# A bias table without its last column, and attention steps weighed two at a time

## The reference

```python
xn = layernorm(x)                                # no scale, no shift
# attention, 16 heads of width 32
q, k, v = heads(xn @ Wq.T), heads(xn @ Wk.T), heads(xn @ Wv.T)
attn = softmax(q @ k.T * 512 ** -0.5)
rel_idx = arange(S)[:, None] - arange(S)[None, :] + (S - 1)      # S = 1024
attn = attn + bias_table[rel_idx]                # added after the softmax
s = layernorm(attn @ v) * gamma + beta
# feed forward, with a spiking neuron of 5 steps behind it
h = square(relu(xn @ W_fc.T))
g = silu(spikes(h @ W_proj.T) / 5)
out = x + s * g
```

## Time and profile before

| | before |
|---|---|
| median of 3 runs | 3528.83 us (3526.05 to 3529.1) |
| span of the profiled execution | 3528.6 us |
| TensorE busy (matmul) | 3421.4 us, 97% |
| ScalarE busy | 2624.2 us, 74% |
| VectorE busy | 2506.6 us, 71% |
| GpSimd busy | 1720.5 us, 49% |
| attention stage | from about 1391 us on |

### The profile page before, as it was taken

How to read it: one execution, slowest core, us unless ns; L and a number is a source line. 1 busy time by engine, 2 the same in 40 slices (tenths; PEclk the granted TensorE clock), 3 DMA queues, 4 the chain that set the end, 5 groups by cost and what they waited for, 6 DMA issues and landing times.

```text
span 3528.6 us, 55344 instructions
## 1 busy us (share of the span) xinstructions
PE 3421.4 (97%) x19961; PEld 1441.3 (41%) x19964; DVE 2506.6 (71%) x4051; ACT 2624.2 (74%) x3898; POOL 1720.5 (49%) x998
## 2 busy tenths in 40 slices
PE   7999999999999999999999999999999999999996
PEld 3444444444444444433433433433433433433431
DVE  5555555555555555777888888888888888888887
ACT  6433333333333335999999999999999999999997
POOL 0012222111111123899666666666666666666672
PEclk9999999999999999999999999999999999999999
DMA  5122322333222222222322322322322322322322
GB/s 186 57 80 80 104 79 80 101 96 103 80 79 79 81 83 86 83 67 72 121 88 84 95 87 83 96 87 84 96 85 83 98 85 82 100 85 82 100 61 84
DMA packets 238752, 312.35 MB, mean 89 GB/s; under 512 B 96624, under 2 KB 132208, under 8 KB 238480
## 3 DMA queue, kind: packets, MB, share of 16 engines
q1 hardware_dynamic: 238480, 308.82, 28.2%
HBM read 174.65 MB, written 76.61 MB: 71 GB/s over the span
## 4 chain that ended last, share of the span: by engine, by line
ACT 33%; PE 11%; issue 10%; DVE 4%; SPq 1%; DMA 1%; ACTq 0%; POOL 0%; DVEq 0%; POOLq 0%
ACT recurrence_or_probs L1457 17%; ACT s_sb L1464 16%; PE misc L1331 3%; PE acc L1406 3%; PE s_ps L1386 3%; PE s_ps L1372 2%; DVE s_sb L1533 2%; DMA xT<-xnT 1%; SPq L322 1%; DVE gate_or_tokens L1662 0%; PE misc L1313 0%; DVE outT L1553 0%; DVE x_or_queries L1570 0%; DVE gate_or_tokens L1665 0%; PE s_ps L1331 0%
## 5 line engine op out<-in xcount | busy, mean ns | idle before, releaser
L1739 POOL TENSOR_TENSOR recurrence_or_probs<-recurrence_or_probs,toep 128x512 f32<-128x512 f32 (+1 forms) x375 | 1288.5, 3457 | 366.5 <-ACT recurrence_or_probs L1457 366.2
L1533 DVE TENSOR_SCALAR_CACHE_REDUCE s_sb<-s_ps 128x1024 f32<-128x1024 f32 x998 | 1213.7, 1220 | 353.8 <-PE s_ps L1372 325.7
L1464 ACT ACTIVATE s_sb<-s_sb,nmax 128x1024 f32<-128x1024 f32 x998 | 1167.0, 1169 | 9.8 <-DVE s_sb L1533 9.5
L1457 ACT ACTIVATE recurrence_or_probs<-s_ps 128x1024 f32<-128x1024 f32 x1024 | 1060.1, 1036 | 7.7 <-PE s_ps L1386 7.5
L559 PE MATMUL ps_fc<-xnT_part,w_fc 128*128 128x512 f16 x3072 | 707.2, 380 | 4.5 <-DVE w_fc L817 4.5
L574 PE MATMUL ps_y<-w_pr,hid_part 128*128 128x512 f16 x3072 | 706.2, 380 | 3.6 <-issue 2.6
L740 ACT ACTIVATE relu<-ps_fc 128x512 f32<-128x512 f32 x256 | 152.7, 597 | 626.9 <-PE ps_fc L559 626.9
L130 POOL TENSOR_TENSOR recurrence_or_probs<-gate_or_tokens,beta_row 128x512 f32<-128x512 f32 x60 | 89.9, 1499 | 1035.3 <-DVE gate_or_tokens L185 1031.7
L929 DVE TENSOR_TENSOR hid<-relu 128x512 f32<-128x512 f32 x256 | 210.3, 822 | 510.9 <-ACT relu L740 510.9
L1406 PE MATMUL acc<-recurrence_or_probs,val 128*32 128x512 f32 x4096 | 545.2, 604 | 2.2 <-DVE recurrence_or_probs L1649 1.5
L559 PEld LDWEIGHTS ps_fc<-xnT_part,w_fc 128*128 128x128 f16 x3072 | 300.6, 98 | 369.3 <-issue 7.8
(11 more groups left out here) (180 smaller groups left out, 2685.1 us busy)
## 6 DMA issues: line engine op xcount, KB each, us to landing
toep<-table_rows SPq DMA_DIRECT2D x32, 2048.0 KB, 8.3
x_or_queries<-x_or_queries SPq DMA_DIRECT2D x384, 64.0 KB, 2.0
x_or_queries<-in_x SPq DMA_DIRECT2D x16, 1024.0 KB, 10.4
xnT<-xnT_part SPq DMA_DIRECT2D x32, 512.0 KB, 8.5
x_or_gate<-in_x SPq DMA_DIRECT2D x16, 1024.0 KB, 9.2
base<-x_or_gate SPq DMA_DIRECT2D x16, 1024.0 KB, 6.8
xT<-xnT SPq DMA_DIRECT2D x32, 512.0 KB, 9.7
result<-gate_or_tokens SPq DMA_DIRECT2D x64, 256.0 KB, 2.0
```

What stands on the lines that cost most here:

```text
L1457: nc.scalar.activation(prob[:, k % PROBS, 2 * second:2 * second + 2, :].rearrange("p j n -> p (j n)"), s_ps[:, item_buffer(pair_item(m)), ...
L1464: nc.scalar.activation(s_sb[:, i % 4, :], s_sb[:, i % 4, :], ACT.Exp, bias=nmax[:, par, j, st:st + 1], scale=-1.0, accum_out=den[:, par, j ...
L1533: nc.vector.tensor_scalar(s_sb[:, i % 4, :], s_ps[:, item_buffer(tile_item(n)), :], -1.0, None, ALU.mult, ALU.min, accum_out=nmax[:, par, ...
L1739: nc.gpsimd.tensor_tensor(tile, tile, toep[:, par, :, at:at + width], ALU.add).then_inc(biased, 1)
```

## The change

The bias of the far keys is taken out of the table: the last column is subtracted from all columns, and the widened part is zero. Its share of the output is then the same for all queries of a batch: the far value times the sum of all values, which is the sum of all tokens times `Wv`. VectorE sums the tokens of each chunk in the feed-forward stage (`sum_tokens`), and 48 small products in slot 0 make the values of all batches and groups (`sum_values`, `take_far_values`); the prefix sums go. The table is grown ahead of the first normalisation and lies in the buffer of relu and its square.

Steps are weighed two at a time, in the second half step of odd steps. Key blocks have a new order in both halves (`KEY_ORDER`), so the added bias widths by step become 512, 128, 512, 256, 512, 384, 512, 512 and then 0, 128, 0, 256, 0, 0, 384, 512 (before 128, 256, 384, 512, 512, 512, 512, 512 and 0, 0, 0, 0, 128, 256, 384, 512). Value projections, the parts of the query and key projection, the rows, one output transpose and the two copies of `acc` have new half steps. The buffers of scores for the sums go from four to three, and the last chunk's gate and base are loaded into `xT`.

```diff
+SUM_TOKENS_AT = {10: 0, 12: 1}
...
-        relu = sb("relu", [P, 2, 512], F32)
-        hid = sb("hid", [P, 2, 512], F32)
+        hidden = sb("hidden_or_table", [P, 2, 2, 512], F32)
+        relu, hid = hidden[:, 0], hidden[:, 1]
...
-        table = sb("table", [rows, d["table_ext"].shape[1]], F32)
+        table = hidden.rearrange("p i a n -> p (i a n)")[:rows, :d["table_ext"].shape[1]]
+        far_row = sb("far_row", [rows, 1], F32)
...
                 wait(sp, xt_stored, (c - 1) * 32)
+                wait(sp, tokens_summed, (c - 1) * 2)
...
-                    sp.wait_ge(table_grown, 1)
-                    sp.dma_start(d["table_ext"], table[:]).then_inc(table_loaded, 16)
-                    sp.wait_ge(table_loaded, 32)
+                    sp.wait_ge(table_stored, 16)
...
             load_x(0)
+            sp.dma_start(table[:, :known], d["tableT"]).then_inc(table_loaded, 16)
             for q in range(4):
                 sp.dma_start(pieces[q], d["fcT"].rearrange("(k p) n -> p k n", p=P)[:, :, q * BANK:(q + 1) * BANK]).then_inc(loaded[q], 16)
+            sp.wait_ge(table_grown, 3)
+            sp.dma_start(d["table_ext"], table).then_inc(table_stored, 16)
             for k in range(4):
                 sp.dma_start(staged[4 + k], d["prT"].rearrange("(k p) n -> p k n", p=P)[:, 4 * k:4 * k + 4]).then_inc(loaded[4 + k], 16)
-            sp.dma_start(table[:, :known], d["tableT"]).then_inc(table_loaded, 16)
...
+                    if n == 0:
+                        act.wait_ge(table_stored, 16)
                     nc.scalar.activation(relu[:, f % 2, :], ps_fc[:, f % 2, :], ACT.Relu).then_inc(relu_done, 1)
...
             def grow_table():
                 dve.wait_ge(table_loaded, 16)
-                nc.vector.tensor_copy(table[:, known:], table[:, known - 1:known].broadcast_to([rows, table.shape[1] - known])
-                                      ).then_inc(table_grown, 1)
+                nc.vector.tensor_copy(far_row[:], table[:, known - 1:known]).then_inc(table_grown, 1)
+                nc.vector.memset(table[:, known:], 0.0).then_inc(table_grown, 1)
+                dve.wait_ge(table_grown, 1)
+                nc.vector.tensor_scalar(table[:, :known], table[:, :known], far_row[:, 0:1], None,
+                                        ALU.subtract).then_inc(table_grown, 1)
+
+            def sum_tokens(c, par, part):
+
+                if part == 0 and c == 0:
+                    dve.wait_ge(xt_hi, 4)
+                    dve.wait_ge(xt_lo, 4)
+                elif part == 0:
+                    dve.wait_ge(xt_turned, c * TURNED)
+                nc.vector.tensor_reduce(spiking.token_sums[:, c * 2 + part, :], xnT[:, par, part], AX,
+                                        ALU.add).then_inc(tokens_summed, 1)
...
+                    if f in SUM_TOKENS_AT:
+                        sum_tokens(c, par, SUM_TOKENS_AT[f])
...
             statistics(0)
+            grow_table()
             normalise(0)
...
-            grow_table()
             chunks(dve, chunk, NC - 2)
...
-VALUES = {0: (0, 0), 2: (0, 1), 4: (1, 0), 6: (1, 1)}
-QUERY_KEYS = {12: (0, 0), 14: (0, 1), 16: (1, 0), 18: (1, 1), 20: (2, 0), 22: (2, 1), 24: (3, 0), 26: (3, 1)}
-SUM_VALUES, ROWS_1, ROWS_0, OUT_1, OUT_0 = 8, 10, 27, 28, 30
+VALUES = {0: (0, 0), 1: (0, 1), 5: (1, 0), 6: (1, 1)}
+QUERY_KEYS = {12 + 4 * u + i: (u, i) for u in range(4) for i in range(3)}
+QK_PARTS = 3
+FAR_VALUES, ROWS_1, ROWS_0, OUT_1, OUT_0 = 9, 10, 28, 29, 30
+KEY_ORDER = ((4, 0, 5, 1, 6, 2, 7, 3), (0, 4, 1, 5, 2, 3, 6, 7))
+COPY_1, COPY_0 = 4, 20
...
+COPIES = 3
...
-        s_sb = sb("s_sb", [P, 4, S], F32)
+        s_sb = sb("s_sb", [P, COPIES, S], F32)
+        last_gate = xT.rearrange("p a k s -> p (a k s)").bitcast(F32).rearrange("p (t i e) -> p t i e", t=4, i=2)
...
         def bias_width(k):
 
-            return min(512, (k % 8 + 1) * P - k // 8 * 512)
+            return min(512, (key_block(k) + 1) * P - k // 8 * 512)
...
-        def last_weighed(b, hg, h):
-
-            k = h // 2 - WEIGH_LAG
-            return (b, hg, k) if k >= 0 else (*before(b, hg), SLOT_STEPS + k)
+        def weighed_at(b, hg, k):
+
+            ready = (k - WEIGH_LAG, k - WEIGH_LAG + 1) if k % 2 else ()
+            return [(b, hg, i) if i >= 0 else (*before(b, hg), SLOT_STEPS + i) for i in ready]
...
-                for n in range(part * 6, part * 6 + 6):
+                for n in range(part * 4, part * 4 + 4):
...
-            def sum_values(s):
+            def sum_values():
 
                 take_misc()
-                pe.wait_ge(consts, CONSTS)
-                pe.wait_ge(v_read, s.g * 2 + 2)
-                for t in range(TB - 1):
-                    last = nc.tensor.matmul(misc[:, :TB], val[:, s.par, t, :], before_key[:, t, :],
-                                            start=(t == 0), stop=(t == TB - 2))
-                last.then_inc(pre_ps, 1)
-                last_use[0] = (pre_read, s.g + 1)
+                pe.wait_ge(sums_split, 3)
+                for hg in range(HG):
+                    for n, (k, a, bb) in enumerate((k, a, bb) for k in range(EB) for a, bb in TERMS):
+                        last = nc.tensor.matmul(misc[:, hg * NB:(hg + 1) * NB], w["v"][:, bb, k, hg * P:(hg + 1) * P],
+                                                batch_parts[:, a, :, k], start=(n == 0), stop=(n == 11))
+                last.then_inc(far_ps, 1)
+                last_use[0] = (far_made, 1)
...
                     if second and (s.main if k >= WEIGH_LAG else s.prev):
-                        weigh(*last_weighed(b, hg, h))
+                        for done in weighed_at(b, hg, k):
+                            weigh(*done)
...
-                wait(dve, sum_done, n - 3)
+                wait(dve, sum_done, n - COPIES + 1)
...
-            def copy_acc(g, par, half):
+            def copy_acc(g, half):
 
                 dve.wait_ge(pv_done, g * 16 + half * 8 + 8)
-                dve.wait_ge(pre_read, g + 1)
+                dve.wait_ge(far_made, 1)
                 wait(dve, tr_ps, g * 2 + half - 1)
-                nc.vector.tensor_tensor(outT[:, half, :].rearrange("p (q n) -> p q n", q=4),
-                                        acc[:].rearrange("p (q n) -> p q n", q=4),
-                                        prefix[:, par, half * 4:half * 4 + 4].unsqueeze(2).broadcast_to([P, 4, P]),
+                nc.vector.tensor_scalar(outT[:, half, :], acc[:], far_values[:, g % HG, g // HG:g // HG + 1], None,
                                         ALU.add).then_inc(acc_read, 1)
...
-                    if h == 2 * WEIGH_LAG and s.prev:
-                        copy_acc(s.g - 1, 1 - s.par, 1)
-                    if h == 2 * WEIGH_LAG + 16 and s.main:
-                        copy_acc(s.g, s.par, 0)
+                    if h == COPY_1 and s.prev:
+                        copy_acc(s.g - 1, 1)
+                    if h == COPY_0 and s.main:
+                        copy_acc(s.g, 0)
```

More of the change, by code:

```diff
@@ L1183, in item_release, with key_block, bias_from @@
             return p_done, m + 1
+        def key_block(k):
+            return KEY_ORDER[k // 8][k % 8]
         def bias_width(k):
-            return min(512, (k % 8 + 1) * P - k // 8 * 512)
+            return min(512, (key_block(k) + 1) * P - k // 8 * 512)
+        def bias_from(k):
+            return TW - P - key_block(k) * P + k // 8 * 512
         def add_count(g, k):
-            return g * 12 + (k + 1 if k < 8 else k - 3)
+            return g * 12 + sum(bias_width(i) > 0 for i in range(k + 1))
         def added_late(g, k):
@@ L1378, in score_pair @@
                 x = pair_item(s.g * 32 + 2 * k + second)
-                half, tb = k // 8, k % 8
-                if tb == 0 and second == 0:
+                half, tb = k // 8, key_block(k)
+                if k % 8 == 0 and second == 0:
                     pe.wait_ge(rows_loaded[half], s.g * 64 + 64)
@@ L1548, in copy_acc, with split_sums @@
-            def copy_acc(g, par, half):
+            def split_sums():
+                sums = spiking.token_sums.rearrange("p (b i) k -> p b k i", b=NB)
+                nc.vector.tensor_reduce(batch_sums[:], sums, AX, ALU.add).then_inc(sums_split, 1)
+                dve.wait_ge(sums_split, 1)
+                nc.vector.tensor_copy(batch_parts[:, 0], batch_sums[:]).then_inc(sums_split, 1)
+                dve.wait_ge(sums_split, 2)
+                nc.vector.tensor_tensor(batch_parts[:, 1], batch_sums[:], batch_parts[:, 0], ALU.subtract).then_inc(sums_split, 1)
@@ L1706, in slot @@
                         finish_statistics(NB * 2 - 2, LAST_STATISTICS[h])
[L1709 to L1712 removed]
+            split_sums()
             slots(dve, slot)
@@ L1715, in _ @@
             newton(NB * 2 - 2)
-            copy_acc(NG - 1, (NG - 1) % 2, 1)
+            copy_acc(NG - 1, 1)
             finish_normalise(NB * 2 - 2, 0)
@@ L1733, in add_bias @@
                     return
[L1734 removed]
+                at = bias_from(k)
                 if k == 0:
```

74 lines of the change are left out of this document (38 added, 36 removed).

## The result

The changed kernel takes 3597.39 us (median of four runs, 3594.62 to 3606.93) against 3527.94 before: a ratio of 1.0202, 95% interval 1.0187 to 1.0216. It was slower, as forecast, but by three times the 22.8 us forecast, and outside the range (3530 to 3566). The profiled execution's span went from 3528.6 to 3597.1 us, 68.5 more.

What follows compares the result with a forecast made beforehand. TensorE was taken to bound the feed-forward stage and ScalarE the attention stage. Terms of 15.0 + 4.0 + 5.3 + 1.0 + 2.0 - 2.7 - 1.8 = 22.8 us gave 3551 us, range 3530 to 3566.

Steps and rivals of the forecast that it cites:

- Key blocks reordered: Adds moved to steps 9 and 11 make TensorE wait for GpSimd at step 13 of slots 0 to 2; 5.3 us.
- term of step 12: Stall at step 12 of even slots stays, as VectorE's stretch keeps its sum; 1.8 us won over thirteen slots.
- Two weighings in one burst: Each burst holds TensorE 1.86 us, 0.14 less than two weighings apart; ScalarE, at its floor, has no use for that.
- The loops through a burst: First exponential to the next through a burst, 4.11 against 4.07 us; four bursts 0.02 late each; with step 3, 4.0 us.
- The slot's start: A burst with two value projections behind it makes a pair late, 0.5 us in each of slots 1 to 30; 15.0 us.
- Token sums: Two VectorE reductions a chunk, 2.3 us each, delay maxima in the last feed-forward chunk; 2.0 us.
- Last chunk's gate: GpSimd's gate operations in slots 0 to 3 delay the add that step 13's burst wants; the 5.3 us of Key blocks reordered.
- Loads of xT: Projections that waited for xT in three slots wait less, as TensorE gets there later; 2.7 us won.
- Far values: 48 small products at half step 9 of slot 0 take 2.7 us and make that loop late; 1.0 us.
- (c): Rival: the second weighing costs its full 1.00 us and turn, 40 us more, 3591 us; chance 0.08.
- (a): Rival: pairs behind bursts are not late, as TensorE is further ahead; 3533 us, no change; chance 0.14.
- (b): Rival: the copy's earlier place ends the stall at step 12, 11.3 us won, about 3518 us; chance 0.08.

Runs made afterwards that it cites:

- e1: The changed kernel with the second half's key blocks back in their old order; 3575.2 us.
- e2: The changed kernel with the first copy of acc back at half step 22; 3598.9 us.
- e9: The changed kernel with one weighing a step, the old half steps, and the second half's key blocks in old order; 3536.3 us.
- e12: e11 with the first half's key blocks in order too and the other even-slot normalisation moved from half step 21 to 24; 3522.2 us.
- e5: The changed kernel with one weighing in each step again and copies of acc at half steps 6 and 22; 3600.1 us.
- e7: The changed kernel with four unread fp16 products of 512 columns at half step 9 of slots 1 to 31; 3585.4 us.
- e3: The changed kernel with the value projections back at half steps 0, 2, 4, 6; 3603.9 us.
- e10: e9 with two weighings in one burst again; 3614.2 us.
- e11: e9 with a 128-column add at step 8, one even-slot normalisation at half step 25, and the last chunk's token sums at its first two steps; 3527.5 us.
- e6: The kernel before with only one of the seven products of the prefix sums; 3528.4 us.
- e4: The changed kernel with seven unread fp32 products of 8 columns at half step 8 of slots 1 to 31; 3602.4 us.

## Why the prediction failed

The direction came as said, but the sum forecast only a third of the loss; two mechanisms that were not in it, and one term that was too small, hold the rest. The two signs of being wrong that the prediction named (a plain slot at 65.8, a first step over 4.8) did not come, with 66.98 and 4.42: they could not show what failed.

- **Key blocks reordered** is the step that failed first. I counted what the moved adds cost in GpSimd's own queue (5.3 us forecast, 5.6 measured) and not what they do to VectorE. The term of step 12, -1.8 us, came out at +19.4 for steps 10 to 12 (e1 gives back 22.7, e2 only 3), and the last slot, counted as 0, at +3.1 (the rows of slot 31; the longer e9 and e12's shorter last slot bear it out).
- **Two weighings in one burst** failed in what it left out. The burst's own price was right (1.86 us to the next pair). What it leaves behind was not looked at: half steps with little but pairs and tiles, behind which the clock falls, 19.4 us (e5 has no such fall and e7 takes 16.0 of them away; the falls in slot 30 were not tested apart). That the clock falls at such a place was in no row I had; that TensorE's work would be thin there, 2.38 of 4.00 us, could be added up.
- **The loops through a burst** were mis-sized: 4.0 us forecast, 12.0 measured. I let only four bursts of a slot be late, by 0.02, though my own loop gave 4.11, and 4.11 is what steps 1, 5, 7, 9, 13 and 15 take (4.07 before). Step 3 is 0.04 longer too, in spite of its logarithm, and the step behind a late pair is 0.02 longer (4.09). Only behind the burst of step 11 is the pair in time (step 12 of odd slots is 4.07).
- **The slot's start** was right in kind and place, 15.0 forecast and 10.6 measured: 0.35 a slot, not 0.5. e3 shows that the reason given for it, two projections in a row, is not the whole one. The burst alone makes steps 0 to 2 longer by 0.58 us together (e10, against e9), and the new projections without it make steps 0 and 2 longer by 0.70 and 0.52 (e5).
- **Token sums** were right in size: 2.28 us each for 2.3, and 2.0 us in the start (1.5 in e9; moved, none in e11 and e12). That the start gave just 2.0 is in part luck: it moves from one execution to the next, 1408.8 to 1411.6 in the nine with the changed first stage and 1405.6 to 1407.7 in three without, 3.5 apart in the means. The neighbours were slowed by GpSimd as well: the instruction of VectorE at 1361.39 takes 1.39 us (0.69 before) and ends 0.54 behind one of GpSimd.
- **Last chunk's gate** (step 13 of slots 0 to 2) was right: 5.6 us, forecast 5.3. **Loads of xT** gave back 3.7, forecast 2.7. **Far values** took 1.35 us, not 2.7, and cost at most 0.4, not 1.0. Prefix sums out: nothing, as said (e6).
- Of the rivals, (c) has a time near the measured one, 3591, and is wrong all the same: a second weighing does not cost 1.00 us. (a) and (b) are out.

Open: how the 22.6 us of first steps and late pairs divide between the burst and the places of the projections, since e5 and e10 show that either without the other costs more; and what of TensorE's work decides that the clock falls in one slot and not in the next, and behind e4's filler but not behind e7's.
